# Router that gives out blocks tile by tile, and gathers that follow eight blocks behind the preceding tile's

## What is computed

```python
logits = x @ gate_w.T                      # 64 experts
topv, topi = jax.lax.top_k(logits, 8)
rw = jax.nn.softmax(topv, axis=-1)
gate, up = x @ gu_w[e], split in 64 + 64   # for each chosen expert e
out = sum_e rw[e] * (silu(gate) * up) @ dp_w[e].T
out = out + sigmoid(x @ g1.T) * shared_expert(x)
```

## Time and profile before

| what | us |
|---|---|
| median of 3 runs (lowest, highest) | 1222.59 (1220.98, 1226.08) |
| the profiled execution | 1226.69 |
| its span, first to last instruction | 1224.9 |
| attention part, to the last batch's last products of scores | 0 to about 671 |
| first matmul of the expert part (L1376) | 758.14 |
| busy in the span: PE, DVE, ACT, Pool | 1029.4, 701.4, 662.9, 647.1 |

### The profile page before, as it was taken

How to read it: one execution, slowest core, us unless ns; L and a number is a source line. 1 busy time by engine, 2 the same in 40 slices (tenths; PEclk the granted TensorE clock), 3 DMA queues, 4 the chain that set the end, 5 groups by cost and what they waited for, 6 DMA issues and landing times. The chain is left out here.

```text
span 1224.9 us, 23397 instructions
## 1 busy us (share of the span) xinstructions
PE 1029.4 (84%) x7305; PEld 813.9 (66%) x7305; DVE 701.4 (57%) x2260; ACT 662.9 (54%) x1586; POOL 647.1 (53%) x883
## 2 busy tenths in 40 slices
PE   3699988898988888989998501999999999999933
PEld 1466665666666656666665401999999999999822
DVE  2476676767767677677673550232246666666642
ACT  1476565665655656556554100666666666666610
POOL 3111123764755847657467775000067777777775
PEclk9799999999989999999998755999999999999965
DMA  2479776821312312212142994677799999999863
GB/s 88 134 249 305 236 248 207 282 99 46 107 57 70 109 43 100 95 48 94 50 134 79 338 305 164 198 226 226 224 311 348 347 349 352 348 348 348 276 191 100
DMA packets 178007, 241.27 MB, mean 197 GB/s; under 512 B 16288, under 2 KB 159712, under 8 KB 176608
## 3 DMA queue, kind: packets, MB, share of 16 engines
q1 hardware_dynamic: 106144, 109.20, 27.7%
q0 software_dynamic: 24576, 69.24, 16.7%
q10 hardware_dynamic: 47168, 61.35, 15.2%
HBM read 107.19 MB, written 132.53 MB: 196 GB/s over the span
## 5 line engine op out<-in xcount | busy, mean ns | idle before, releaser
L1468 POOL DMA_INDIRECT yk<-res_d,slot_i x240 | 232.3, 968 | 209.3 <-DMA res_d<-y 137.1
L456 POOL DMA_INDIRECT rows_d<-pay,slot_i x256 | 256.9, 1003 | 73.4 <-issue 68.4
L861 DVE TENSOR_REDUCE nmax<-ps 128x1 f32<-128x512 f32 (+3 forms) x448 | 225.8, 530 | 103.3 <-PE ps L511 101.0
L729 ACT ACTIVATE wgu_s<-ps 128x512 f32<-128x512 f32 x320 | 191.7, 600 | 95.0 <-PE ps L511 91.3
L1195 DVE SCALAR_TENSOR_TENSOR inner<-inner,picked,psB 128x64 f32<-128x64 f32 x320 | 75.3, 277 | 186.4 <-ACT inner L1277 186.4
L511 PE MATMUL ps<-mask,ident_b 128*128 128x256 bf16 (+1 forms) x640 | 173.3, 271 | 0.0
L504 PE MATMUL ps<-kT,qT 96*128 96x512 f32 (+3 forms) x512 | 167.4, 389 | 6.8 <-DVE nmax L861 4.5
L1386 PE MATMUL psB<-wgu_s,xT 128*128 x1276 | 170.5, 277 | 0.8 <-ACT xT L1272 0.8
L1403 PE MATMUL psD<-wdp_s,innerT 128*128 x638 | 165.2, 381 | 0.0
L551 PE MATMUL ps<-qT,kT 128*128 128x512 f32 (+3 forms) x512 | 162.7, 380 | 0.8 <-ACT qT L742 0.6
L1386 PEld LDWEIGHTS psB<-wgu_s,xT 128*128 128x128 f32 x1276 | 156.7, 193 | 1.2 <-issue 1.2
(11 more groups left out here) (253 smaller groups left out, 1571.6 us busy)
## 6 DMA issues: line engine op xcount, KB each, us to landing
rows_d<-blank ACTq DMA_DIRECT2D x8, 5440.0 KB, 19.4
xg<-rows_d SPq DMA_DIRECT2D x160, 272.0 KB, 4.7
res_d<-y SPq DMA_DIRECT2D x159, 256.0 KB, 4.2
wgu_s<-wgu_in ACTq DMA_DIRECT2D x8, 1024.0 KB, 14.2
x_d<-x SPq DMA_DIRECT2D x30, 192.5 KB, 2.9
xs<-x_d SPq DMA_DIRECT2D x30, 192.5 KB, 4.0
wgu_s<-x_in SPq DMA_DIRECT2D x32, 128.0 KB, 2.1
rows_d<-pay,slot_i POOLq DMA_INDIRECT x256
```

The lines of the kernel that those rows point to most:

```text
L456: pool.indirect_dma_start(rows_d, bass.IndirectOffsetOnAxis(ap=slot_i[:, b, t, k:k + 1], axis=0), pay[par][:, t, :], None).then_inc(s_scat ...
L729: act.activation(pexp[p % 4][:, s, :], ps2[:, (5 * p + s) % 2, :], ACT.Exp, scale=HEAD_D ** -0.5).then_inc(s_exp, 1)
L861: return dve.tensor_reduce(nmax[u][:, tile, heads[0]:heads[-1] + 1], src, AX.X, ALU.max, negate=True)
L1468: pool.indirect_dma_start(yk_at(tile)[:, k], None, res_d[0:min(USED, 2 * stored_before(tile)) * P, :], bass.IndirectOffsetOnAxis(ap=slot_i ...
```

## The change

The router works with five columns for four tiles where it had one for the batch. New blocks of an expert are given out tile by tile: the counts run on over the tiles (`psq[0:EXPERTS, t:TILES]`), the sums over experts come in a chain over the tiles, `open` (the base of the expert's last opened block) is a running maximum over tiles, and the diagonal tile holds 3 x 4 x 64 columns in place of 3 x 64. Products at k = 7 and a new step of PE at k = 9 (which waits for ACT's copy) take the place of the broadcasts. `complete` counts 8 blocks for each tile so far, and 63; so `stored_before` of tile 0 is 36 pairs in place of 48, every tile asks for its rows, all have four steps, and two tiles are late in place of four. The diff, without the constants' signs and the renamed columns:

```diff
+            wide = sb("wide", [P, 3, TILES, EXPERTS], F32)
+            diag = wide[0:EXPERTS]
+            thd, place, left = wide[:, 0], wide[:, 1], wide[:, 2]
@@ route_columns @@
+                    chained(eng.tensor_scalar(c(PART), c(COUNT + 1), P / 2 - 0.5, 1.0 / P, ALU.add, ALU.mult), 1)
+                    chained(eng.tensor_scalar(c(PART), c(PART), 2.0 ** 23, None, ALU.add), 2)
+                    chained(eng.tensor_scalar(c(ROOM + 1), c(PART), -(2.0 ** 23), float(P), ALU.add, ALU.mult), 3)
+                    eng.tensor_tensor(c(NEW), c(ROOM + 1), c(ROOM), ALU.subtract).then_inc(s_new, 1)
-                    chained(eng.tensor_scalar(c(12), c(0), c(2), 1.0, ALU.add, ALU.add), 4)
-                    chained(eng.tensor_scalar(c(13), c(1), c(2), 1.0, ALU.add, ALU.add), 5)
...
                     eng.wait_ge(s_base, b + 1)
-                    chained(eng.tensor_tensor(c(10), c(8), c(1), ALU.subtract), 6)
-                    chained(eng.tensor_tensor(c(14), c(10), c(2), ALU.subtract), 7)
-                    eng.tensor_tensor(diag[:], (identity, 3 times), c(12, 3) (broadcast), ALU.mult).then_inc(s_diag, 1)
-                    chained(eng.tensor_tensor(c(9), c(8), c(7), ALU.add), 8)
-                    chained(eng.tensor_scalar(c(11), c(7), 0.0, c(14), ALU.is_gt, ALU.mult), 9)
-                    chained(eng.tensor_tensor(c(2), c(2), c(11), ALU.add), 10)
-                    chained(eng.tensor_copy(c(0), c(4)), 11)
-                    chained(eng.tensor_copy(c(1), c(6)), 12)
+                    chained(eng.tensor_tensor(c(HIGH), c(START), c(ROOM), ALU.subtract), 4)
+                    chained(eng.tensor_scalar(c(PART), c(HIGH), 1.0 / P, -1.0, ALU.mult, ALU.add), 5)
+                    chained(eng.tensor_tensor(c(FAR), c(PART), c(NEW), ALU.mult), 6)
+                    for t in range(TILES):
+                        chained(eng.tensor_scalar(c(OPEN + 1 + t, 1), c(FAR + t, 1), c(OPEN + t, 1), None, ALU.max), 7 + t)
+                    chained(eng.tensor_scalar(c(PART), c(OPEN), 1.0, None, ALU.add), 11)
+                    chained(eng.tensor_tensor(c(SHIFT), c(HIGH), c(PART), ALU.subtract), 12)
+                    eng.tensor_tensor(c(SHIFT + TILES), c(COUNT), c(PART), ALU.add)
+                    eng.tensor_tensor(c(SHIFT + 2 * TILES), c(COUNT), c(ROOM), ALU.subtract)
+                    chained(eng.tensor_scalar(c(SHIFT), c(SHIFT), float(1 - P), None, ALU.add), 13)
+                    eng.tensor_tensor(diag, (identity, 3 * TILES times), c(SHIFT, 3 * TILES) (broadcast),
+                                       ALU.mult).then_inc(s_diag, 1)
+                    chained(eng.tensor_tensor(c(MARK), c(NEW), c(START), ALU.mult), 14)
+                    chained(eng.tensor_scalar(c(MARK), c(MARK), 1.0 / P, None, ALU.mult), 15)
+                    (copies of COUNT, ROOM and OPEN, the last chained as 16)
@@ PE, k = 3 @@
+                        pe.matmul(psq[0:EXPERTS, 0:TILES + 1], cst[0:EXPERTS, C_TRI:C_TRI + EXPERTS],
+                                  col[:, NEW:NEW + TILES + 1], start=True, stop=False, skip_group_check=True)
+                        for t in range(TILES):
+                            last = pe.matmul(psq[0:EXPERTS, t + 1:TILES + 1], ones_f[0:EXPERTS, 0:EXPERTS],
+                                             col[:, NEW + t:NEW + t + 1].to_broadcast([EXPERTS, TILES - t]), ...
@@ PE, k = 7 and 9 @@
                         pe.wait_ge(s_diag, b + 1)
+                        pe.matmul(psq[:, 256:512], ones_f[0:EXPERTS, :], diag[:, 0], start=True, stop=True)
+                        pe.matmul(psq[:, 0:256], ones_f[0:EXPERTS, :], diag[:, 1], start=True, stop=False)
-                        (the 128 and 256 column products of diag, and three products of chosen by ones_b)
                         last = pe.matmul(psq[:, 0:TILES * EXPERTS], tri_b[:], chosen[:], ...
+                    if k == 9:
+                        pe.wait_ge(s_thd, b + 1)
+                        pe.matmul(psq[:, 256:512], ones_f[0:EXPERTS, :], diag[:, 2], start=True, stop=False)
+                        pe.matmul(psq[:, 256:512], tri_b[:], chosen[:], start=False, stop=True).then_inc(s_room_ps, 1)
@@ DVE, k = 8 and 9 @@
+                        dve.wait_ge(s_pool, ROUTE_CHAIN * b + 15)
+                        for t in range(TILES):
+                            dve.scalar_tensor_tensor(out=taken[:], in0=blk, scalar=col[:, MARK + t:MARK + t + 1],
+                                                     in1=taken[:], op0=ALU.is_equal, op1=ALU.add).then_inc(s_tk, 1)
+                        dve.wait_ge(s_room_ps, b + 1)
+                        dve.scalar_tensor_tensor(out=place, in0=beyond, scalar=0.0, in1=thd,
+                                                 op0=ALU.is_ge, op1=ALU.mult).then_inc(s_pl, 2)
-                        (the same by two operations)
@@ expert part @@
-                return min(BLOCKS, (tile // TILES + 1) * SEQ * TOP // P + EXPERTS - 1)
+                return min(BLOCKS, (tile + 1) * TOP + EXPERTS - 1)
-                return stored_before(tile) + DOWN + GATHERED_AFTER + every(tile) // 2 * (tile % TILES) + k * every(tile) // 2 // TOP
+                return stored_before(tile) + DOWN + GATHERED_AFTER + k // 2
-            assert late_sums == list(range(ALL_TILES - TILES, ALL_TILES))
+            assert late_sums == [ALL_TILES - 2, ALL_TILES - 1]
-                    if tile % TILES == 0:
-                        rows_stored(tile)
+                    rows_stored(tile)
-                rows_stored(LATE)
-                pool.wait_ge(e_back, backs(step_of[GATE][PAIRS - 1]))
                 for tile in late_sums:
+                    rows_stored(tile)
```

More of the change, by code:

```diff
@@ L201, in build @@
             SCATTER_AT = 13
[L202 removed]
+            ROUTE_AT, ROUTE_PARTS, ROUTE_CHAIN = 1, 12, 16
             FIRST_EVERY = 3
@@ L276, in route_columns @@
                 b = h * 2 + par
-                c = lambda k, n=1: col[:, k:k + n]
+                c = lambda k, n=TILES: col[:, k:k + n]
                 def chained(ins, step):
                     ins.then_inc(s_pool, 1)
-                    eng.wait_ge(s_pool, b * STEPS + step)
+                    eng.wait_ge(s_pool, b * ROUTE_CHAIN + step)
                     eng.sem_inc(waits_met)
-                STEPS = 12
                 if k == 0:
@@ L652, in route @@
                         for t in range(TILES):
-                            last = pe.matmul(psq[0:EXPERTS, 0:1], chosen[:, t, :], ones_b[:, 0:1],
-                                             start=(t == 0), stop=(t == TILES - 1))
+                            last = pe.matmul(psq[0:EXPERTS, t:TILES], chosen[:, t, :], ones_b[:, t:TILES],
+                                             start=(t == 0), stop=(t == TILES - 1), skip_group_check=True)
                         last.then_inc(s_cnt_ps, 1)
@@ L679, in route @@
                         last.then_inc(s_rank_ps, 1)
+                    if k == 9:
+                        pe.wait_ge(s_thd, b + 1)
+                        pe.matmul(psq[:, 256:512], ones_f[0:EXPERTS, :], diag[:, 2].rearrange("p t e -> p (t e)"),
+                                  start=True, stop=False, skip_group_check=True)
+                        pe.matmul(psq[:, 256:512], tri_b[:], chosen[:].rearrange("p t e -> p (t e)"),
+                                  start=False, stop=True, skip_group_check=True).then_inc(s_room_ps, 1)
                 program(pe, {"pre": pre, "main": main, "products": products, "post": post, "route": route})
@@ L966, in route @@
                         dve.wait_ge(s_pl, 4 * b + 3)
-                        dve.tensor_tensor(place[:], place[:], chosen[:], ALU.mult).then_inc(s_pl, 1)
+                        dve.tensor_tensor(place, place, chosen[:], ALU.mult).then_inc(s_pl, 1)
                     if k == 10:
@@ L1040, in complete @@
             def complete(tile):
-                return min(BLOCKS, (tile // TILES + 1) * SEQ * TOP // P + EXPERTS - 1)
-            def every(tile):
-                return 6 if tile // TILES == BATCH - 2 else 8
+                return min(BLOCKS, (tile + 1) * TOP + EXPERTS - 1)
             def stored_before(tile):
@@ L1156, in _ @@
                 assert tile == LATE
-                for tile in (LATE + 2, LATE + 3, LATE, LATE + 1):
+                for tile in late_sums:
                     if tile >= LATE + 2:
@@ L1353, in _ @@
                 pe.wait_ge(s_thd, BATCH)
-                pe.wait_ge(s_tk, 4 * BATCH)
-                pe.matmul(psA[:, 0, 0:BLOCKS], pidx_neg, taken[:], start=True, stop=True).then_inc(e_own_ps, 1)
+                pe.wait_ge(s_tk, 5 * BATCH)
+                pe.matmul(psA[:, 0, 0:BLOCKS], pidx, taken[:], start=True, stop=True).then_inc(e_own_ps, 1)
                 pe.wait_ge(e_offs, 1)
```

83 lines of the change are left out of this document (35 added, 48 removed).

## The result

| what | us |
|---|---|
| before, median of 4 runs (lowest, highest) | 1222.39 (1220.98, 1226.08) |
| after, median of 4 runs (lowest, highest) | 1246.76 (1245.47, 1252.36) |
| ratio, 95% interval | 1.0203 (1.0164 to 1.0242) |
| the profiled execution of after, its span | 1245.47, 1243.3 |
| first matmul of the expert part (L1386 of after) | 806.67 |

A forecast was written before the change was run, and what follows sets the result against it. PE was taken to bound the attention part, Pool's start and pace the end. Gathers -29.0, six routers +35.7, batch 6 +3.9 and batch 7 +5.2 made +15.8 us, a median of about 1238 us, range 1223 to 1252.

The forecast's parts named there:

- The gathers: Expert part: Pool's first gather waits for 36 stored pairs, not 48, so the last comes earlier: -29.0 us.
- The stall: Routers of batches 0 to 5: PE stands waiting for Pool's later diagonal, 3.85 us each, bounds 3.7 and 4.3.
- The clock: Batches 0 to 5: the stall brings one 0.02 drop of granted clock, 1.3 us a beat, bounds 0 and 2.6.
- rival C: Attention beats: the clock falls twice, 1.3 us more in each router, 1246 us; chance 9%.
- The rest of the router: Batches 0 to 5, each: third step's products 0.1, ninth step on PE 0.3, DVE's marks and wide operations 0.4 us.
- Batches 6 and 7: Batch 6's router on Pool between scatters, +3.9 us; batch 7's on DVE, without slack, +5.2 us.
- The sum: Whole kernel: gathers, six routers and batches 6 and 7 together +15.8 us, median about 1238 us.
- The signs: Profile: PE waits 3.5 to 4.5 us, beats 85 to 87, diagonal 1.7 to 2.2, first gather after 105, end 7.6.
- A: Attention beats swallow the stall, six routers cost about 1 us each, 1209 us; chance 9%.
- B: Attention beats: part of the stall and no clock drop, six routers 25 us, so 1228 us; chance 13%.
- D: Expert part: gathers don't start earlier, most of the 29 us is missing, 1255 to 1267 us; chance 7%.

The follow-up runs named there:

- e2: The kernel before with 15 more dependent one-column operations on Pool ahead of the diagonal; 1275.68 us, ratio 1.0413.
- e9: e6 with 28 needless products of 256 columns ahead of the wait for the diagonal in batch 6 alone; 1208.42 us, ratio 0.9868.
- e6: e5 with VectorE's reading of the block bases moved from the router's fifth step (k == 4) to its fourth; 1208.12 us, ratio 0.9877.
- The two doses: e2 and e2b, the kernel before with 15 and 9 added Pool operations ahead of the diagonal; 1275.68 and 1255.73 us.
- the filled stalls: Needless products ahead of the wait for the diagonal: 36 in the changed kernel (e3), 1229.46 us; 16 in e5's kernel, 1214.07 us.
- e1: The changed router with the old gathers (48 stored pairs before the first, four late tiles); 1278.23 us, ratio 1.0432.
- e5: The changed kernel with a shorter column chain on Pool and a third of the diagonal written beforehand; 1228.90 us, ratio 1.0046.
- e2b: The kernel before with 9 more dependent one-column operations on Pool ahead of the diagonal; 1255.73 us, ratio 1.0269.
- e3: The changed kernel with 36 needless products of 256 columns ahead of PE's wait for the diagonal, batches 0 to 5; 1229.46 us, ratio 1.0047.
- e8: e6 with 16 needless products of 256 columns ahead of the wait for the diagonal, batches 0 to 5; 1211.48 us, ratio 0.9894.

## Why the prediction was right in sign and short by 8.6 us

**The gathers** (-29.0): right. In the medians they gave 31.5 us, by the recorded ratios 28; in the profiles the way from the first matmul of the expert part to the last gather fell from 459.1 to 429.1 us, by 30.0. My 29.0 lies among these. Pool's wait on stored rows fell from 135.6 to 104.0 us, 31.6 where twelve steps make 29.0; 2.0 us came back because the first tile's gathers now take 12.2 us and no longer 10.1. That Pool is the limit again, with the last gather 7.6 us before the end, was right (7.5). 16 late gathers were enough.

**The stall** (3.85, bounds 3.7 and 4.3): the mechanism was right and the sum short by 0.7. The chain took 5.61 us, not 4.58. In batch 5, where no step is stretched, it took 4.69, so nearly all of the error is the two stretched steps: I had taken each step's time from rows in which none is. Such a row had been there: before's L315, one addition of a column, was busy for 0.18 to 0.61 us over its six turns. The diagonal went the other way, 1.47 us for 768 columns where I took 1.8 and none of my bounds reached so low. The Trainium skill, GPSIMD Engine Reference (8. Key points), says that GpSimd shares its SBUF interfaces with VectorE and contends with its instructions that have two SBUF inputs. By that rule the stretched steps are those beside L851 and L856, and the trace agrees: 0.59 and 0.80 us there in batches 0 to 4, 0.19 and 0.27 in batch 5, where these DVE operations are missing. It is not the whole rule, though. Pool's timeline of e2, a one-column step beside such an operation (L842, at 286.35 to 286.82) and one without:

```profile
286.65 0.24 POOL L310 TENSOR_SCALAR col<-col 64x1 f32<-64x1 f32 x1 [0.20 <-POOL col L308]
...
287.48 0.20 POOL L310 TENSOR_SCALAR col<-col 64x1 f32<-64x1 f32 x1 [0.19 <-POOL col L310]
```

A step beside L847 took 0.23. These are hardly longer; why the steps of after suffer so much more is open. The estimate of 1.7 us for the diagonal, worked out from the figure in section 3.1 of the same page, was too high by 0.2 as well.

**The clock** (1.3 a beat, bounds 0 and 2.6): mis-sized. The price of one drop of 0.02 held: beats of e9 and e6 at 1.00, 0.98 and 0.96 took 79.3, 80.1 and 81.8 us. Their number did not: I let a stall bring one, and the granted clock of the five beats fell from 0.96 to 0.92, two. The two doses give 1.9 us a beat, the filled stalls up to 2.9. It is the term that rival C named, at 1.3 more a beat. The Trainium skill, TensorE: Matmul & The Clock Gate (What's actually happening), has the half rate as the default, from which activity releases the array. By that rule a long wait is followed by slow products until the array has been busy again, and the trace agrees: behind 4.53 us of standing the masked product took 0.44 us at 294.11 and 0.29 at 297.80.

**The rest of the router** (0.1 + 0.3 + 0.4 = 0.8 a beat): right, as far as beats can tell. e6, which keeps nearly all of it and has 0.26 us of stall, is 0.7 us a beat above before. Together: 4.53 + 1.9 + 0.7 = 7.1 us of the 7.7 that a beat grew by, where I had 5.95; the remaining 0.6 is inside what two executions differ by.

**Batches 6 and 7** (+3.9 and +5.2): the mechanism of the second was wrong. I read "released by DVE's slots" at Pool's scatter of 707.42 as the first scatter of batch 7 and concluded that there was no slack. It was one of the last five scatters of batch 6, which Pool still had to issue. Pool's timeline of after, with its last scatter of batch 6 and its first of batch 7, and DVE's slots of batch 7:

```profile
760.32 0.96 POOL L464 DMA_INDIRECT rows_d<-pay,slot_i  x1 [0.30 <-issue]
762.05 0.96 POOL L464 DMA_INDIRECT rows_d<-pay,slot_i  x1 [0.77 <-issue]
...
760.71 0.18 DVE L328 TENSOR_SCALAR slot_i<-slot_f 128x32 int32<-128x32 f32 x1
```

In before the 32nd scatter from the end stands at 713.74 (the last at 752.96), and the slots were ready at 707.35: 6.4 us of slack, which took up all but 0.5 us of the longer router. From the first scatter behind batch 6's columns (658.22 in before, 706.10 in after) to the very last one it is 94.74 us in before and 95.14 in after, at Pool's pace in both. So 5.2 of the sum were not there. For batch 6 itself the terms of my sum make +3.8, not +3.9. Of the 48.5 us by which the attention part grew in the profiles, six routers at 7.7 us leave 2.3 for both batches, where I had 9.1; an estimate, since the six are taken from five beats.

**The sum.** Measured from the medians: routers +55.8, gathers -31.5, together +24.4, against +44.8 and -29.0. In the profiles the attention part grew by 48.5 us (51.3 in e1); before's profiled execution lay 4.3 us above its median and after's 1.3 below, and I had let before's 4 us stand for both. That is 5.6 of the 8.6 us. The other 3 are what is left of larger errors against each other: six beats 10.5 us too short, batches 6 and 7 6.8 us too long. That the sum came so near is in part luck.

**The signs.** The wait of 4.53 us, its releaser, the distance of the first gather and the end were as named or nearly so. Two were not: a beat takes 88.6 us, not 85 to 87, and the diagonal 1.47, not 1.7 to 2.2.

**The rivals.** A and B are out: no beat absorbed any of the stall, with 6.6 us for 4.69 in the cleanest case (e2). C (9%, 1246 us) had the clock right, two drops in place of one; that its time came out to within 1 us is luck, since its sum kept a stall that was too short and the 5.2 us of batch 7. D is out: all idle time of Pool on stored rows but the first is 6.7 us over 15 waits.

## What to carry to other kernels

A wait of the busiest engine costs more than its length, since its clock falls with it: here about 1.9 us on top of each stall, for 2.3 us as for 4.7. Where other engines bound the stage (batch 6, e9), filling the wait won nothing. So price a new step on an off-path engine by the slack at the place where the busy engine waits for it, and if that slack is exceeded, start the chain earlier or shorten it until nothing is left; half a repair (e5) left 20 us on the table. And before a step is called on or off the path by the releaser that a row names, count the instructions still queued ahead of it.

## What the runs showed of the hardware

- TensorE's granted clock fell to half after waits of 1.78 us (e5) and 2.27 us (e2b), not only after 4.5. The products behind the wait then took 1.05 us for 0.59 and 0.44 for 0.28.
- Needless bf16 products kept the clock at its upper level through a wait (e3: 17.3 us won for 4.09 us of products in each of six beats), and cost 3.4 us in all, not 11, where there was no wait (e8); at the same granted clock the beat was longer by all of their 1.8 us.
- Two small operations of Pool's chain took 0.59 and 0.80 us beside DVE operations with two SBUF inputs (after, batches 0 to 4) and 0.19 and 0.27 without them (batch 5). One-column steps beside the like in e2 took only 0.24 for 0.20.
- Pool's multiplication of 64x768 took 1.47 us, of 64x512 1.04 and of 64x192 0.50 to 0.56; DVE's of 64x768 0.95.
